# A relational graph layer's gates computed as row dot products on VectorE, and its turned features cut into two parts straight from PSUM

## What is computed

```python
def rgcn_gate_layer(x, row, col, edge_type, basis, att, gate_w, root, bias):
    w = jnp.einsum('rb,bio->rio', att, basis)        # 30 basis matrices, 2 relations
    x_j = x[col]
    for r in range(2):
        gate = sigmoid(x_j @ gate_w[r, :, 0])        # one number per node and relation
        msgs.append(gate[:, None] * x_j @ w[r])
    msg = where(edge_type == 0, msgs[0], msgs[1])
    return segment_sum(msg, row) + x @ root + bias

h = relu(rgcn_gate_layer(x, ..., basis1, att1, gate_w1, root1, bias1))
out = rgcn_gate_layer(h, ..., basis2, att2, gate_w2, root2, bias2)
```

## Time and profile before

| | us |
|---|---|
| median of 3 runs | 513.11 |
| the runs | 507.73, 513.11, 513.49 |
| the profiled execution, device time | 511.62 |
| its span, first to last instruction | 509.8 |
| mean granted TensorE clock | 0.973 of full speed |

### The profile page before, as it was taken

One profiled execution on the slowest core, in us unless ns is written; L12 is line 12 of the kernel. 1 busy time (PEld: TensorE's weight loads), 2 busy tenths in 40 slices (PEclk: granted clock), 3 DMA queues, 4 the chain that ended last, 5 costly groups with the idle time before them and its releaser, 6 DMA issues.

```text
span 509.8 us, 6126 instructions
## 1 busy us (share of the span) xinstructions
PE 460.1 (90%) x2210; PEld 278.8 (55%) x2214; DVE 334.3 (66%) x721; ACT 234.4 (46%) x415; POOL 20.4 (4%) x43
## 2 busy tenths in 40 slices
PE   1699999988797888999998997998798999999997
PEld 1343343433342343874455765686275788877885
DVE  4787887799986798815769666665879253930222
ACT  3797795666784724232122435534543632531210
POOL 3210000001000000100010000000000000000000
PEclk9999999999997999999999999899898999988999
DMA  7983354007999856945069866442986040000002
GB/s 279 342 325 126 121 187 153 33 1 295 397 374 419 341 217 231 420 173 186 0 219 391 318 254 235 181 177 79 415 321 212 22 158 9 1 1 1 0 1 84
DMA packets 18457, 98.16 MB, mean 193 GB/s; under 512 B 3711, under 2 KB 4095, under 8 KB 7935
## 3 DMA queue, kind: packets, MB, share of 16 engines
q1 hardware_dynamic: 14871, 73.58, 38.1%
q0 software_dynamic: 3552, 24.12, 12.4%
HBM read 92.45 MB, written 5.24 MB: 192 GB/s over the span
## 4 chain that ended last, share of the span: by engine, by line
PE 70%; DMA 15%; DVE 9%; ACT 3%; issue 2%; SPq 1%; DVEq 0%
PE bank L1175 13%; DMA bring<-in_basis 13%; PE sbank L1484 9%; PE bank L1244 6%; PE sbank L1161 6%; PE bank L1497 6%; PE sbank L1227 6%; PE bank L1392 5%; PE bank L1469 5%; PE bank L1211 3%; DMA alph<-in_alphas 3%; PE sbank L1351 2%; PE bank L1161 2%; DVE s L885 2%; PE sbank L1145 2%
## 5 line engine op out<-in xcount | busy, mean ns | idle before, releaser
L1161 PE MATMUL sbank<-bring,attw 120*32 120x512 f32 x320 | 41.9, 634 | 3.8 <-DMA bring<-in_basis 3.8
L711 DVE TENSOR_SCALAR cnt<-iota_row,edge_f 128x512 bf16<-128x512 f16 x132 | 40.7, 343 | 4.5 <-PE sbank L1227 4.5
L1096 DVE SCALAR_TENSOR_TENSOR y_lo<-sbank,gate,y_hi 128x512 fp32r<-128x512 f32 x16 | 12.0, 751 | 35.7 <-ACT y_hi L635 35.7
L374 ACT ACTIVATE stat<-stat 128x1 f32<-128x1 f32 x32 | 6.5, 202 | 59.5 <-DVE stat L719 59.5
L404 ACT ACTIVATE s<-bank,colsb 128x512 f32<-128x512 f32 x24 | 16.5, 688 | 36.0 <-PE bank L1175 36.0
L1227 PE MATMUL sbank<-cnt,adjT 128*128 128x512 bf16 x128 | 29.4, 382 | 1.9 <-DVE cnt L711 1.3
L1244 PE MATMUL bank<-hT,wring 128*128 128x512 f32 x64 | 30.2, 617 | 0.0
L461 ACT ACTIVATE adjT<-distance,edge_w,edge_f 128x128 bf16<-128x128 bf16 x61 | 29.2, 480 | 1.4 <-PE sbank L1227 1.4
L1161 PE MATMUL bank<-bring,attw 120*32 120x512 f32 x192 | 23.8, 618 | 6.3 <-DMA bring<-in_basis 6.3
L635 ACT ACTIVATE y_hi<-sbank,gate 128x512 fp32r<-128x512 f32 x16 | 11.0, 688 | 39.8 <-PE sbank L1484 39.8
L436 ACT ACTIVATE distance<-iota_row,edge_f 128x128 bf16<-128x128 f16 x61 | 24.4, 400 | 5.1 <-DVE edge_f L755 3.5
(11 more groups left out here) (207 smaller groups left out, 1029.8 us busy)
## 6 DMA issues: line engine op xcount, KB each, us to landing
bring<-in_basis SPq DMA_DIRECT2D x63, 1024.0 KB, 8.1
wring<-in_weights POOLq DMA_DIRECT2D x8, 1024.0 KB, 9.4
w_scratch<-stage SPq DMA_DIRECT2D x64, 64.0 KB, 6.4
hT<-in_weights POOLq DMA_DIRECT2D x4, 1024.0 KB, 5.1
landing<-in_weights POOLq DMA_DIRECT2D x4, 1024.0 KB, 8.5
qkw<-w_scratch POOLq DMA_DIRECT2D x2, 2048.0 KB, 8.9
rring<-in_rows POOLq DMA_DIRECT2D x12, 256.0 KB, 7.7
xr<-in_x SPq DMA_DIRECT2D x4, 256.0 KB, 3.9
```

The lines of the kernel that those rows point to most:

```text
L711: dve.tensor_scalar(hot_s[:, n % HOT, :], iota[:, :], src_f[:, n:n + 1], None, ALU.is_equal).then_inc(sem("hot_ready"), 1)
L1161: mm = pe.matmul(unit_bank(b)[32 * j:32 * j + 32, :], attw[0:KB, u // UNITS, g, :], bring[0:KB, u % BATCH, j, :], start=(g == 0), stop=(g ...
```

## The change

The gate columns no longer go through PE with the turned features. Instead, ahead of the layer, PE spreads each gate vector over all partitions: `gate_row(i)`, i = 0..3 (two relations, two layers), is four f32 matmuls of 128 x 128 x 128 whose stationary operand is one gate column broadcast to 128 columns and whose moving operand is the identity. The result, 512 values, the same in each partition, lands in bank 4 or 5 and is copied by ACT into `gate_rows` (which reuses `hT`). DVE then takes the gate logits as dot products along the free axis, 8 instructions a layer with an accumulator as second output, and ACT applies one sigmoid per layer. As `hT` is no longer needed for gates, `rel_turn` casts PSUM straight to `xT_hi`, and `xT_lo` subtracts from PSUM.

```diff
+        gate_rows = hT
+        gate_sum = sb("gate_sum", [P, 2, C, RELS])
 # ACT, after the last batch_norm and stage_units(1)
+                        for i in range(2 * RELS):
+                            act.wait_ge(sem("gate_rows_psum"), i + 1)
+                            act.copy(gate_rows[:, i, :], bank[4 + i % 2][:, :]).then_inc(sem("gate_rows"), 1)
-                def gates(layer, c):
-                    act.wait_ge(sem("gates_psum"), layer * C + c + 1)
-                    act.activation(gate[:, layer, c, :], bank[4 + c % 2][:, 0:RELS], ACT.Sigmoid).then_inc(
+                def gates(layer):
+                    act.wait_ge(sem("gates"), RELS * C * (layer + 1))
+                    act.activation(gate[:, layer, :, :], gate_sum[:, layer, :, :], ACT.Sigmoid).then_inc(
                         sem("sigmoid"), 1)
                 def rel_turn(layer, c):
-                    act.copy(hT[:, :, blk(P, c)], turned).then_inc(sem(f"relT{layer}"), 1)
-                    act.wait_ge(sem(f"relT{layer}"), c + 1)
-                    act.copy(xT_hi[:, :, blk(P, c)], hT[:, :, blk(P, c)]).then_inc(sem("xT_hi"), 1)
+                    act.copy(xT_hi[:, :, blk(P, c)], turned).then_inc(sem("xT_hi"), 1)
 # ACT's order, layer 0
-                gates(0, 0)
-                gates(0, 1)
                 stage_units(2)
                 rel_turn(0, 2)
                 rel_turn(0, 3)
                 split_w(0, 0)
-                gates(0, 2)
-                gates(0, 3)
                 split_w(0, 1)
+                gates(0)
 # ACT's order, layer 1
                 for c in range(C):
                     rel_turn(1, c)
-                    gates(1, c)
+                gates(1)
 # DVE: xT_lo = PSUM - xT_hi (was hT - xT_hi)
+                def gates(layer):
+                    for rel in range(RELS):
+                        dve.wait_ge(sem("gate_rows"), layer * RELS + rel + 1)
+                        for c in range(C):
+                            dve.wait_ge(sem("h_rel0" if layer == 0 else "rel0_out"), c + 1)
+                            dve.wait_ge(sem("gates"), layer * RELS * C + rel * C + c)
+                            dve.scalar_tensor_tensor(s0[:, c, :], hr[:, c, :], 1.0, gate_rows[:, layer * RELS + rel, :],
+                                                     ALU.mult, ALU.mult,
+                                                     accum_out=gate_sum[:, layer, c, rel:rel + 1]).then_inc(
+                                                         sem("gates"), 1)
                 split_w(0, 0)
                 split_w(0, 1)
+                gates(0)
                 dve.tensor_copy(cnt_r[0][:, :, :], cnt[:, 0, :, :]).then_inc(sem("cnt_r"), 1)
 ...
                 xT_lo_part(1, C - 1)
+                gates(1)
                 Y_lo(1, 0)
 # PE, ahead of and behind the last batch norm's transposes
+                def gate_row(i):
+                    if i >= 2:
+                        pe.wait_ge(sem("gate_rows"), i - 1)
+                    for k in range(C):
+                        mm = pe.matmul(bank[4 + i % 2][:, blk(P, k)],
+                                       col(f"gw{i // RELS + 1}", k * RELS + i % RELS).to_broadcast([P, P]),
+                                       ident[:, :], start=(k == 0), stop=(k == C - 1), skip_group_check=True)
+                    mm.then_inc(sem("gate_rows_psum"), 1)
+                need_parts("c2_1")
+                gate_row(0)
+                gate_row(1)
                 pe.wait_ge(sem("c2_1"), C)
 ...              # the x4 transposes
+                gate_row(2)
+                gate_row(3)
                 units(4)
 # PE: gates(layer, c) and its eight calls are gone
                 def turn_rel(layer, ready, c):
                     if c >= 2:
-                        pe.wait_ge(sem("sigmoid"), layer * C + c - 1)
+                        pe.wait_ge(sem("xT"), layer * C + c - 1)
 # PE, Y_tiles, first relation
-                        pe.wait_ge(sem("sigmoid"), (layer + 1) * C)
+                        pe.wait_ge(sem("xT"), (layer + 1) * C)
```

## The result

| | before | after |
|---|---|---|
| median of 5 runs, us | 513.11 | 499.02 |
| runs, us | 507.73 to 514.25 | 495.80 to 502.05 |
| ratio | | 0.9741 (95%: 0.9703 to 0.9779) |
| profiled execution, its span, us | 511.62, 509.8 | 495.80, 494.0 |
| mean granted clock | 0.973 | 0.989 |

The median fell by 14.1 us, and by the ratio 513.11 x 0.0259 = 13.3 us; 12.2 off the execution and a median of 500.5 were forecast. The profiled executions differ by 15.8 us, but not all of that is the change: ACT's last batch norm pass starts at 357.37 in the one and at 354.42 in the other, and up to there both kernels do the same work, but for the two gate rows that PE does while it waits for ACT. These 3 us are there already at 180 us, in the attention part. In the twelve other profiles this point lies between 353.79 and 357.98. So I compare stretches inside an execution, not spans, from here on.

A forecast was written before the change was run, and what follows sets the result against it. PE, 70% of the chain, was taken as the bound. 3.26 + 5.56 + 3.40 = 12.2 us off the profiled 511.62 gave 499.4; the median was put 1.1 above, at 500.5, range 497 to 503.

The forecast's parts named there:

- gates off PE, layer 0: Layer 0's gate matmuls, which lay in PE's chain between matmuls that don't wait, go: 3.26 us off.
- gates and their waits off PE, layer 1, and the clock: Layer 1's two stretches of gates and waits go, 5.56 us, and its slow root matmuls regain full clock, 3.40 us.
- of this the clock: Layer 1's root matmuls behind the two gate stretches no longer run at low clock: 3.40 us off.
- new `xT` waits: Turning blocks 2 and 3 now waits for `xT_lo` of blocks 0 and 1; hidden under `rel_root`, cost nothing.
- p, one product of DVE: One DVE gate product with accumulator read and semaphore: 0.92 us, bounds 0.73 and 1.57; eight a layer.
- stall at `Y_tiles(0, 1)`: PE waiting in layer 0 for the first `Y_lo`, queued behind DVE's products: taken as 0, called the tight place.
- one gate row: PE's four f32 matmuls spreading one gate vector ahead of the layer: 1.09 us, bounds 0.79 and 1.75.
- stages ahead of the layer: Gate rows hide behind PE's waits for ACT and DMA: 0 us added; DVE's chain there had 0.2 us slack.
- sum: Whole kernel: 3.26 + 5.56 + 3.40 = 12.2 us off, nothing added.
- 8p - 7.3: Layer 0's stall in front of `Y_tiles(0, 1)` for product time p: nothing to 0.1 us at 0.92, 5.2 at 1.57.
- the shape with two non-bf16 SBUF sources runs at half throughput: Rival, chance 0.09: DVE products with accumulator are slow, 1.57 us each, `Y_tiles(0, 1)` stalls 5.2 us, time 505.7.
- The clock rival: Rival, chance 0.12: layer 1's clock falls even without gates, so only 8.8 us off, 503.8 us.

The follow-up runs named there:

- before_b: The kernel before, unchanged, profiled a second time; the losses of its two slow root groups in layer 1 add up to 3.7 us.
- rows2: The kernel after with each gate row's matmuls made twice; last batch norm pass to last matmul 137.23 us, against 136.00 in the kernel after.
- thin24: The kernel after plus 12 two-column f32 matmuls behind layer 1's first root group; from that group's end to the first Y tile 13.33 us, against 9.12.

## Why the prediction was right, step by step

| step | predicted, us | measured, us |
|---|---|---|
| gates off PE, layer 0 | 3.26 | 3.5 (30.12 less 26.59, low clock behind the hole in both; 29.60 less 26.06, full in both) |
| gates and their waits off PE, layer 1, and the clock | 5.56 + 3.40 = 8.96 | 9.1 to 10.0 (58.33, 59.10, 58.16 less 49.06) |
| of this the clock | 3.40 | 3.4, 3.7, 3.2 on the root groups in the three traces of before; in `before_b` also 0.45 on a turn |
| new `xT` waits | 0 | 0 (root groups at 2.75 to 2.77) |
| p, one product of DVE | 0.92 | 0.80 |
| stall at `Y_tiles(0, 1)` | 0 | 0, with 1.1 to spare |
| one gate row | 1.09 | 1.02 |
| stages ahead of the layer | 0 | 0, beside the chance of the aggregation's clock |
| sum | 12.2 | 12.8 (124.75 less 111.93, low clock behind the hole); 13.9 and 12.7 (125.30, 124.06 less 111.39 of `rows2`, full clock) |

**The mechanism held at each step that the runs could tell apart.** The time came out some 0.5 to 1.7 us better than the sum, inside the range. About 0.5 of it lies in the root groups. In layer 0 the two groups right behind gates took 2.87 and 2.89 us even at full clock and take 2.76 and 2.74 now; in layer 1 the clock's 3.40 was reckoned from a group of 2.83 us, and a group takes 2.74 to 2.77 now. What was mis-sized is p: the accumulator read was taken from ACT's 185 ns and takes 80 ns on DVE. That 0.1 us, eight times, is most of the 1.1 us that layer 0 had to spare where the forecast had it at nothing to 0.1. A product doubled to 1.52 us stalled PE by 4.91, and 8p - 7.3 gives 4.9 for it: the rule was good and only its entry was off.

One sum of the prediction is off by a little: 12.2 - 3.4 = 8.8 us off gives 503.9 by its own step to the median, not 503.8.

The Trainium skill's statement that an accumulator output is an instruction of its own (VectorE: DVE Perf Modes, "Two Vector instructions with no wait between them"): the trace agrees, it shows 16 of them. Its rule that the shape with two non-bf16 SBUF sources runs at half throughput (Vector Engine (DVE) Microarchitecture Reference, "Points that are easy to get wrong"), which was a rival: the product with an accumulator and two f32 sources takes 0.69 us, as the plain form does. The measurement decides; it is not so here.

**The clock rival** (the clock falls anyway) had the question right: with the gates gone no root group of layer 1 took more than 2.82 us in any profile but that of `thin24`, which puts thin work back. The prediction's reason, that the clock falls after long thin stretches, is shown for thin work of 2.58 us. For the stretches of the kernel before, which were part thin work and part waiting, it is half of the reason: 16 thin records without the waiting did not do it. The 3.40 holds either way.

**What the prediction did not see** is the chance in the aggregation. It named the DVE chain there as the risk, correctly (`rows2`), but took the kernel before's 7.50 us as fixed; two more profiles gave 8.53 and 9.15. The clock behind the hole ahead of the first turn is another such chance, of 0.5 us. By all that these profiles show, both belong to the spread of the runs and not to the change.

## What to carry to other kernels

A matmul of a few columns on a turned block costs PE its weight load, makes PE wait for the block to be turned, and the clock can fall behind it; of the 12.2 us that the gates were forecast to cost here, a little over half was their own time on PE. Where the untransposed operand is at hand, a dot product on DVE with an accumulator costs 0.80 us per 128 x 512. It is off the path as long as it ends before the first reader of what it scales: count what is queued behind it on its engine. PE is not rid of all the work: spreading the four gate vectors cost it 4.1 us, free here because it stands where PE waited anyway. And after such a change look for the next hole: two lists that handed a block on only after the next one's statistics kept 3.5 us on the path. Before two single profiles are compared, look at the places where the clock comes and goes by chance in the same kernel.

## What the runs showed of the hardware

- DVE's accumulator read took 0.08 us, ACT's 0.185; a chained product with its read had 0.80 us start to start.
- 2.58 us of two-column f32 matmuls (24 records) were followed by clock 0.65 over the next 4.9 us; 1.68 us of them (16) and 2.50 us of 512-column f32r matmuls were followed by 1.00, in one profile each. Of the two levels, 1.2 and 2.4 GHz, only the first group behind ran mostly at the lower one.
- 16 such records with 0.74 or 1.15 us of standing still among them had the lower level behind them, or from their last part on, in six of six stretches of the kernel before; 16 without it, in its layer 0, in none of three.
- PE standing still for 4.91 us was followed by clock 0.57. Standing still for 1.90 us ahead of the first turn was followed by the lower level in six of eleven profiles and by the full one in five.
- The same program had its aggregation at 7.61 us in one execution and 9.10 in another.
